# The hidden values of a mixture of experts: turned by TensorE, or in 32x32 squares by VectorE and joined through DRAM

## The reference

```python
g = jnp.einsum('nd,efd->enf', xf, W_gate)
u = jnp.einsum('nd,efd->enf', xf, W_up)
y = jnp.einsum('enf,edf->end', jax.nn.silu(g) * u, W_down)
...
for k in range(TOP_K):
    out = out + y[top_idx[:, k], n_ar] * pi[:, k:k + 1]
```

## Time and profile before

| | |
|---|---|
| median of 3 runs | 2131.14 us (2129.84 to 2132.89) |
| span of the profiled execution | 2131.7 us |
| its own time | within the range of the runs above; the span is 0.6 us over their median |
| TensorE, VectorE, ScalarE, GpSimd busy | 92%, 56%, 65%, 38% of the span |
| experts, from the first turned rows to the last product | 722 to 1422 us |
| mean granted clock of TensorE | 0.952 |

### The profile page before, as it was taken

How to read it: one execution, slowest core, us unless ns; L and a number is a source line. 1 busy time by engine, 2 the same in 40 slices (tenths; PEclk the granted TensorE clock), 3 DMA queues, 4 the chain that set the end, 5 groups by cost and what they waited for, 6 DMA issues and landing times. The chain is left out here.

```text
span 2131.7 us, 37883 instructions
## 1 busy us (share of the span) xinstructions
PE 1951.8 (92%) x12223; PEld 1128.9 (53%) x12223; DVE 1184.9 (56%) x2130; ACT 1378.3 (65%) x1586; POOL 804.1 (38%) x704
## 2 busy tenths in 40 slices
PE   6989999999946699999999999968899999999998
PEld 5722333333342488888888888856622222222255
DVE  4511135345667623433333332337599999999967
ACT  5689999999923133233233233226699999999934
POOL 2000111111110242443342443211078888988922
PEclk9999999999965699999999999989899999999999
DMA  6744234444110520211202220229845434363012
GB/s 197 237 108 70 46 74 90 90 79 87 44 41 5 223 101 28 87 45 69 92 21 92 90 85 26 85 111 332 286 66 117 84 57 117 58 151 66 13 78 71
DMA packets 76901, 203.66 MB, mean 96 GB/s; under 512 B 13068, under 2 KB 28174, under 8 KB 74600
## 3 DMA queue, kind: packets, MB, share of 16 engines
q1 hardware_dynamic: 68632, 181.51, 31.8%
q0 software_dynamic: 6816, 18.62, 2.6%
q10 hardware_dynamic: 1248, 0.92, 0.2%
HBM read 338.84 MB, written 60.03 MB: 187 GB/s over the span
## 5 line engine op out<-in xcount | busy, mean ns | idle before, releaser
L1326 PE MATMUL psum<-A_qa,A_ka 50*128 50x512 f32 x2048 | 409.0, 468 | 22.8 <-DVE A_qa L1413 6.2
L1326 PEld LDWEIGHTS psum<-A_qa,A_ka 50*128 50x128 f32 x2048 | 177.0, 186 | 471.4 <-DVE A1f_probs L1423 242.9
L2513 PE MATMUL psum<-e_w_high,e_xT 128*128 x1136 | 386.8, 402 | 3.8 <-DVE e_xT L2463 3.8
L1547 POOL TENSOR_TENSOR A1f_probs<-A1f_probs,A1f_bias 128x512 f32<-128x512 f32 x256 | 327.5, 1291 | 81.3 <-ACT A1f_probs L1378 80.9
L1423 DVE SCALAR_TENSOR_TENSOR A1f_probs<-psum,A1f_bias 128x1024 f32<-128x1024 f32 x256 | 311.6, 1217 | 23.6 <-PE psum L1326 20.0
L2470 DVE TENSOR_TENSOR e_hT<-psum,e_hT 128x1024 fp32r<-128x1024 f32 x71 | 86.9, 1224 | 421.7 <-ACT e_hT L2434 421.7
L1366 ACT ACTIVATE A0f_probs<-psum 128x1024 f32<-128x1024 f32 x256 | 313.9, 1226 | 3.5 <-PE psum L1326 3.5
L1378 ACT ACTIVATE A0f_probs<-psum 128x1024 f32<-128x1024 f32 x256 | 316.1, 1235 | 0.0
L1345 PE MATMUL psum<-A1f_probs,v 128*32 128x512 f32 x2048 | 274.1, 606 | 17.5 <-POOL A1f_probs L1547 16.5
L1370 ACT ACTIVATE A1f_probs<-A1f_probs 128x1024 f32<-128x1024 f32 x256 | 273.9, 1070 | 4.7 <-DVE A1f_probs L1423 3.7
L1345 PE MATMUL psum<-A0f_probs,v 128*32 128x512 f32 x2048 | 274.3, 608 | 0.0
(11 more groups left out here) (292 smaller groups left out, 2627.2 us busy)
## 6 DMA issues: line engine op xcount, KB each, us to landing
e_w_raw<-in_experts SPq DMA_DIRECT2D x73, 3072.0 KB, 11.7
qk_parts<-L_part SPq DMA_DIRECT2D x64, 512.0 KB, 4.0
A_qa<-qk_parts SPq DMA_DIRECT2D x192, 128.0 KB, 4.2
A_ka<-qk_parts SPq DMA_DIRECT2D x192, 128.0 KB, 6.3
om<-results SPq DMA_DIRECT2D x16, 512.0 KB, 7.5
A1f_bias<-tables SPq DMA_DIRECT2D x16, 384.0 KB, 7.7
A1f_bias<-tables SPq DMA_DIRECT2D x16, 320.0 KB, 10.3
L_x<-in_x SPq DMA_DIRECT2D x8, 512.0 KB, 7.6
```

The source lines that it names most:

```text
L1326: mm = e.matmul(ps[:, side * HALF:(side + 1) * HALF], self.qk.ka[rows, s, pair, kt * P:(kt + 1) * P].bitcast(FP32R), self.qk.qa[rows, s, p ...
L1547: e.tensor_tensor(fourth, fourth, self.bias_of(*w[1:], slice(self.FOURTH, GH)).rearrange("p h q -> p (h q)"), ALU.mult).then_inc(self.mult ...
L2513: mm = e.matmul(out, left[part].bitcast(FP32R), moving.bitcast(FP32R), start=start and i == 0, stop=stop and i == 2)
```

## The change

For tiles 0 to 68 (BY_PE = 69) TensorE turns the hidden values no more. VectorE turns them in squares of 32x32 (square), SyncE stores the result to DRAM (store_squares) and loads it back in four DMAs, one for each 32 partitions, so that the squares come to stand as in the turned matrix (load_turned). The order of hidden values on partitions and blocks differs from before, and the down weights are laid out to match. The last two tiles still go through TensorE. ScalarE's and VectorE's splits read the loaded copy in SBUF, which has two buffers. The down product is two tiles behind (LAG = 2). The Silu is written into e_hid, which takes e_act's place.

SyncE's stream now consists of the stores and loads of hidden values, so the fetches of weights move to ScalarE's queue, behind the Silu, in pieces of at most 4096 columns; that of the fourth expert moves to GpSimd. GpSimd's low part is split in two, up (4096 columns) and down (2048, one pass later), as are ScalarE's signals for the high part. Two of the four pieces of x are fetched at the end of the stage. Route's six semaphores between VectorE and TensorE become two; its work is the same and is left out below.

```diff
+    LAG = 2
+    BY_PE = MOE_TILES - LAG
+    Q, R = 4, 32
...
-        self.act_sb, self.hid = sb("e_act", [P, F]), sb("e_hid", [P, F])
+        self.hid = sb("e_hid", [P, F])
         self.hT, self.y = sb("e_hT", [P, 2, FC, P]), sb("e_y", [P, Y_BUFS, D])
+        self.squares, self.turned = sb("e_squares", [P, F]), sb("e_turned", [P, 2, F])
...
-        return 3 if j == "second" else j + 1 if j < 2 else j + 2
+    def second_ready(self, j):
+        return 2 * j - 1
+    def up_ready(self, j):
+        return 2 * j
+    def down_ready(self, j):
+        return 2 * j + 3
...
+        self.fetch(e, 0, SECOND, 0, self.second_in)
         e.wait_ge(self.first_low, 3)
-        beside(e)
-        fetch(1, THIRD, 0, self.weights_in)
-        for j in range(1, MOE_TILES):
-            if j == 2:
-                e.wait_ge(self.low_ready, self.low_value("second"))
-                fetch_fourth(0, False)
-            e.wait_ge(self.low_ready, self.low_value(j))
-            fetch_fourth(j, True)
+        beside(e, (2, 3))
+        self.fetch(e, 1, THIRD, 0, self.weights_in)
+        for j in range(self.BY_PE):
+            self.store_squares(e, j)
+            self.load_turned(e, j)
         e.wait_ge(self.second_in, DMA)
...
+        e.wait_ge(self.weights_in, DMA * (MOE_TILES - 1 - self.LAG))
+        e.wait_ge(self.h_low, self.BY_PE)
+        beside(e, (0, 1))
+    def store_squares(self, e, j):
+        e.wait_ge(self.squared, j + 1)
+        if j >= 2:
+            e.wait_ge(self.turned_in[j % 2], self.Q * DMA * (j // 2))
+        e.dma_start(self.hidden_dram[j % 2, :, :], self.squares[:, :]).then_inc(self.squares_out, DMA)
+    def load_turned(self, e, j):
+        e.wait_ge(self.squares_out, DMA * (j + 1))
+        if j >= 2:
+            e.wait_ge(self.h_low, j - 1)
+        n = F // self.Q
+        rows = self.hidden_dram[j % 2, :, :].rearrange("(a r) n -> r a n", r=self.R)
+        for q in range(self.Q):
+            e.dma_start(self.turned[q * self.R:(q + 1) * self.R, j % 2, :].rearrange("r (a n) -> r a n", n=n),
+                        rows[:, :, q * n:(q + 1) * n]).then_inc(self.turned_in[j % 2], DMA)
...
+        def low_of(buf, a, b):
+            e.tensor_tensor(self.w.low[:, buf, a:b].bitcast(FP32R), self.w.raw[:, buf, a:b], self.w.high[:, buf, a:b],
+                            ALU.subtract)
+        def low_second(j):
+            e.wait_ge(self.high_ready, self.second_ready(j))
+            is_new = self.planned(e, IS_NEW, 1)
+            with e.If(is_new > 0 if j == 1 else is_new < 1):
+                low_of(slice(0, 1), 0, WIDE)
...
+                self.fetch(e, 0, FOURTH, 0, self.fourth_in)
+            e.drain().then_inc(self.low_ready, 1)
...
+        def low_part(j, a, b, value):
+            e.wait_ge(self.high_ready, value)
...
+            is_new = self.planned(e, IS_NEW, j)
+            with e.If(is_new > 0):
+                low_of(buf, a, b)
             e.drain().then_inc(self.low_ready, 1)
...
-                low_part(0, 1, j == 1, 1 if j == 1 else 3)
+                low_second(j)
             if j + ROW_BUFS < MOE_TILES:
                 self.load_rows(e, j + ROW_BUFS)
+            if j >= self.LAG:
+                self.store_y(e, j - self.LAG)
             if j >= 1:
-                self.store_y(e, j - 1)
-                low_part(j, j, True, self.low_value(j))
-        self.store_y(e, MOE_TILES - 1)
+                low_part(j, 0, DOWN_AT, self.up_ready(j))
+            if j >= self.LAG:
+                low_part(j - 1, DOWN_AT, WIDE, self.down_ready(j - 1))
+        for j in range(MOE_TILES - self.LAG, MOE_TILES):
+            self.store_y(e, j)
+        e.wait_ge(self.fourth_in, DMA)
         for o in range(Y_BUFS):
...
-        def high_part(j, a, b, got, value, flag=None, is_set=True):
+        def high_of(buf, a, b):
+            e.activation(self.w.high[:, buf, a:b].bitcast(FP32R), self.w.raw[:, buf, a:b], ACT.Copy)
...
+        def high_second(j):
...
+                e.wait_ge(self.second_in, DMA)
+                high_of(slice(0, 1), 0, WIDE)
+            e.drain().then_inc(self.high_ready, 1)
...
+            is_new = self.planned(e, IS_NEW, j)
+            with e.If(is_new > 0):
+                e.wait_ge(self.weights_in, DMA * min(max(1, j - 1), MOE_TILES - 1 - self.LAG))
+                if j >= 2:
+                    e.wait_ge(self.fourth_in, DMA)
+                high_of(buf, a, b)
+            e.drain().then_inc(self.high_ready, 1)
+        def fetch_fourth(j):
+            e.wait_ge(self.low_ready, self.down_ready(j))
+            e.dma_start(self.w.raw[:, bass.ds(self.planned(e, OTHER_BUFFER, j), 1), :],
+                        self.w.weights[bass.ds(self.planned(e, FOURTH, j), 1), :, :].rearrange("e p n -> p e n"),
+                        cond=self.planned(e, IS_NEW, j) > 0, max_dma_last_dim=WEIGHT_RUN).then_inc(self.weights_in, DMA)
...
+            self.wait_turned(e, j)
             if j:
                 e.wait_ge(self.downed, j)
-            e.activation(self.hT[:, 0, :, :].rearrange("p f n -> p (f n)").bitcast(FP32R), self.HT,
-                         ACT.Copy).then_inc(self.h_high, 1)
+            high, whole = self.parts_of_hidden(j, 0)
+            e.activation(high, whole, ACT.Copy).then_inc(self.h_high, 1)
         for j in range(MOE_TILES):
             if j in (1, 2):
-                high_part(0, 0, WIDE, self.second_in, DMA, flag=1, is_set=(j == 1)).then_inc(self.high_ready, 1)
+                high_second(j)
+            if j >= self.LAG:
+                split_hidden(j - self.LAG)
             e.wait_ge(self.gated, j + 1)
-            if j:
+            if j > self.BY_PE:
                 e.wait_ge(self.hidden, j)
-            e.activation(self.act_sb[:, :], self.GU[:, 0, :], ACT.Silu).then_inc(self.silu, 1)
+            elif j:
+                e.wait_ge(self.squared, j)
+            e.activation(self.hid[:, :], self.GU[:, 0, :], ACT.Silu).then_inc(self.silu, 1)
+            if self.LAG < j < MOE_TILES - 1:
+                fetch_fourth(j - self.LAG)
             if j >= 1:
-                value = DMA if j == 1 else DMA * (j + 1)
-                split_hidden(j - 1)
                 e.wait_ge(self.upped, j)
-                high_part(j, 0, DOWN_AT, self.weights_in, value)
-                move_y(j - 1)
-                high_part(j, DOWN_AT, WIDE, self.weights_in, value).then_inc(self.high_ready, 1)
-        split_hidden(MOE_TILES - 1)
-        move_y(MOE_TILES - 1)
+                high_part(j, 0, DOWN_AT)
+            if j >= self.LAG:
+                move_y(j - self.LAG)
+                high_part(j - 1, DOWN_AT, WIDE)
+        for j in range(self.BY_PE, MOE_TILES):
+            split_hidden(j)
+            move_y(j)
+    def wait_turned(self, e, j):
+        if j < self.BY_PE:
+            e.wait_ge(self.turned_in[j % 2], self.Q * DMA * (j // 2 + 1))
+        else:
+            e.wait_ge(self.h_turned, j - self.BY_PE + 1)
+    def parts_of_hidden(self, j, part):
+        out = self.hT[:, part, :, :].bitcast(FP32R)
+        if j >= self.BY_PE:
+            return out.rearrange("p f n -> p (f n)"), self.HT
+        squares = {"a": P // self.R, "f": FC}
+        return out.rearrange("p f (a s) -> p a f s", a=P // self.R), self.turned[:, j % 2, :].rearrange(
+            "p (a f s) -> p a f s", **squares)
...
+            low, whole = self.parts_of_hidden(j, 1)
...
+                "p f (a s) -> p a f s", a=P // self.R)
...
+            e.tensor_tensor(low, whole, high, ALU.subtract).then_inc(self.h_low, 1)
...
+            e.wait_ge(self.silu, j + 1)
+            e.wait_ge(self.upped, j + 1)
+            out, parts = self.hid[:, :], (self.hid[:, :], self.GU[:, 1, :])
+            if j >= self.BY_PE:
+                if j == self.BY_PE:
+                    e.wait_ge(self.squares_out, DMA * j)
...
+            e.tensor_tensor(out, *parts, ALU.mult).then_inc(self.hidden, 1)
+        def square(j):
+            e.wait_ge(self.hidden, j + 1)
+            if j:
+                e.wait_ge(self.squares_out, DMA * j)
+            e.transpose(self.squares[:, :], self.hid[:, :]).then_inc(self.squared, 1)
...
-            if j >= 1:
-                rest_of_hidden(j - 1)
-            e.wait_ge(self.silu, j + 1)
-            e.wait_ge(self.upped, j + 1)
-            if j:
-                e.wait_ge(self.h_turned, j)
-            e.tensor_tensor(self.hid[:, :], self.act_sb[:, :], self.GU[:, 1, :], ALU.mult).then_inc(self.hidden, 1)
             if j + 1 < MOE_TILES:
                 split_rows(j + 1)
+            if j >= self.LAG:
+                rest_of_hidden(j - self.LAG)
+            multiply(j)
+            if j < self.BY_PE:
+                square(j)
             if j >= 8:
                 next(beside, None)
-        rest_of_hidden(MOE_TILES - 1)
+        for j in range(self.BY_PE, MOE_TILES):
+            rest_of_hidden(j)
...
-            if j:
+            if j > self.BY_PE:
...
             for f in range(FC):
```

(30 more changed lines are left out.)

97 lines of the change are left out of this document (44 added, 53 removed).

## The result

The changed kernel takes 2268.97 us (median of 4 runs, 2265.24 to 2274.3) against 2130.49 for the one before (4 runs, 2128.84 to 2132.89): a ratio of 1.0652, 95% interval 1.0635 to 1.0669. Slower, as forecast, but by 138.5 us where 70 were forecast, and past the end of the range (2260). The profiled execution has a span of 2266.9 us at a mean granted clock of 0.922.

The account below looks back on a forecast made before the run. The prediction took TensorE's stream to bound the experts and summed 2131.7 - 60.7 (transposes) + 99 (new experts) + 7 (clock) + 21.6 (start) + 2 (end) = 2200.6, forecasting 2200 us, range 2108 to 2260.

Parts of the forecast that it names:

- The transfers, 3.0 and 4.5 us: Hidden values through DRAM: the store takes 3.0 us, the four loads 4.5 from first issue; the round trip is hidden.
- The ring: ScalarE's fetch waits for GpSimd's previous tile, whose store needs ScalarE's y move: 8.0 us of a tile's 8.60.
- A: Rival: the ring decides, as worked out: 2200 us, own range 2150 to 2245; chance 0.60.
- A stall of 9 us will do the same; the ring hides most of it, I take 1 us each: TensorE's clock falling to 0.50 behind new experts' stalls: 7 us in all, bounds 0 and 3 each.
- ScalarE's split and VectorE's subtraction read SBUF in place of PSUM ... still beside TensorE's work: Hidden values' split and subtraction keep 1.02 and 1.22 us, twice that at worst, hidden beside TensorE's work.
- The gaps of the experts, 15 each: TensorE's lateness at each of seven new experts, 15 us where 0.8 before: +99 us, bounds 10 and 20 each.
- Quiet tiles with 0.6 us to spare: Tiles without new weights lose nothing, since the ring takes 8.0 of 8.60 us.
- rival C: The ring also delays quiet tiles, as result landings grow from 2.4 to 3.5 us: 2228, or 2250; chance 0.15.
- Start, +21.6: Stage's start: GpSimd's fetch and drain for the fourth expert delay tile 2: +21.6 us, 9.9 if the drain doesn't wait.
- Rival B: The ring stays open if GpSimd's part ends by about 5 us: faster, 2073 or 2108 us; chance 0.17.
- Rival D: DRAM round trip late, at fetches (2235 us) or in each tile (69 us per us late); chance 0.04.
- Rival E: No change within 0.2%, with new experts 8 us late and a cheap start: 2133 us; chance 0.04.

Follow-up runs that it names:

- e1: The kernel before, with only the conditional fetch of weights moved to ScalarE behind the Silu and a wait for GpSimd's part: 2391.0 us, ratio 1.1231.
- e2: The changed kernel, with the fetch behind the Silu of tile j being that of tile j-4 in place of j-2: 2174.4 us, ratio 1.0214.
- e3: The changed kernel, with GpSimd's low parts made in instructions of 1024 columns: 2269.7 us, ratio 1.0667.
- e5: e2, with ScalarE also copying the loaded hidden values into PSUM, from where VectorE subtracts in tiles up to 65: 2131.6 us, ratio 1.0004.
- e10: e2 with e3's pieces, third product waiting for older down weights, third and fourth experts' fetches on ScalarE in tiles 4 and 7, x at the end: 2133.6 us.
- e11: e10, with e5's operand in PSUM in place of e3's pieces on GpSimd: 2126.0 us, ratio 0.9976.

## Why the prediction was right in sign and wrong in size

- **Transposes, 0.88 us each:** right. Undisturbed third products stand 8.59 apart, 0.89 less.
- **VectorE's turn, 1.22:** right, 1.25. **The transfers, 3.0 and 4.5 us:** right away from fetches; the store lands in 2.9, and the loads are never waited for in a quiet tile.
- **The ring as the likeliest case (A):** right. e1 has the wait and none of the squares or transfers, and e2 takes the wait away and 94.6 us with it. Its walk through a new expert was close: 15 us forecast, 16.6 us of gaps in the mean of e3, where the hold is 3.3 us at most (and GpSimd's parts longer by the pieces).
- **"A stall of 9 us will do the same; the ring hides most of it, I take 1 us each":** the step that failed, and half of what the forecast was off by. 40.8 us were lost beyond the gaps where 7 stood in the sum, 5.8 each, past its bound of 3; 34.5 of them are half of the 69.0 us at clock 0.50. The ring does not hide it, since it runs through the third product, which takes 5.0 us in place of 3.1 behind a gap; and at most experts the second or third gap brings the clock down once more. No run sets the clock by itself, so this share is read from the traces and not shown by an experiment.
- **"ScalarE's split and VectorE's subtraction read SBUF in place of PSUM ... still beside TensorE's work":** the step whose mechanism failed. A second SBUF operand made the subtraction wait for GpSimd's, 8.93 us. In the change the ring covers it: without the hold the gaps are 12.7 us less and the time is the same (e3). So it is not what put the change past the range; without the ring it is worth 43 us (e2 to e5).
- **The gaps of the experts, 15 each:** 18.1, inside their bounds of 10 to 20; 21.9 us more than forecast in all.
- **Quiet tiles with 0.6 us to spare:** too hopeful, and part of rival C came true. Landings of results grew from 2.4 to 3.1, reads on ScalarE took longer, moves of y often stand 9.0 to 9.8 apart, and 10.4 us are lost.
- **Start, +21.6:** right, +22.8, with a first gap that the prediction did not have. The first hidden store lands after 14.8 us, behind weights and x in SyncE's queue (e10 shows it), and the subtraction is then held, 8.04 us: together a gap of 19.4. The second gap, 10.0, ends with the forecast chain, behind GpSimd's drain of 13.2 us. This chain sets the sum: in e3 the first gap is 12.9 and the second 16.1, 28.9 for 29.4. **End, +2:** 3.3.
- **Rival B** failed by its own condition: GpSimd's subtraction ended 16.3 us after the last free third product (1151.9 to 1168.25; the forecast's walk had 13.7), not by 5. **Rival D**, a late round trip at fetches, did not show in the change past the start, because the ring was longer; it is a part of what is left once the ring is gone (e11). **Rival E** needed new experts at 8 us and a cheap start, and neither came.
- **The range** reached to each rival alone, 2260. What is over the forecast, 68.6 us by the account, is 33.8 beyond the gaps, 21.9 in them, 10.4 in quiet tiles, and 2.5 at start and end. A itself (to 2245) was left by the term for the clock; the quiet tiles came on top.

So the gain of 60.7 us is real on TensorE and was given back, first to the ring, behind it to VectorE's hold, and behind that to transfers beside the weights. Open is whether the last can be had: no run kept the fetch of weights away from the hidden stores.

## What to carry to other kernels

A wait that nobody suffers from (528.8 us on SyncE's queue) is not free to move: ask what stands behind it in the new queue, and follow it around until it meets itself. Where two causes cover the same stretch, taking away the shorter one shows nothing; test them together and one by one. And when an operand moves from PSUM to SBUF, look at what GpSimd runs meanwhile, even if the instruction's own price stays.
